# Graph convolutions on one Trainium2 core: 28 of 784 edge tiles fetched row by row from SyncE and ScalarE, and a ring of 72 slots

## The reference, cut to what matters

```python
def gcn_conv(x, W, b, src, dst, num_nodes):
    h = x @ W
    s = jnp.concatenate([src, loop]); d = jnp.concatenate([dst, loop])
    dinv = rsqrt(deg)
    msg = h[s] * (dinv[s] * dinv[d])[:, None]
    return jax.ops.segment_sum(msg, d, num_segments=num_nodes) + b
...
x = gcn_conv(layernorm(x), W1, b1, src, dst, 6250)
x = relu(x)
x = gcn_conv(x, W2, b2, src, dst, 6250)
```

## Time and profile before

| | us |
|---|---|
| runs | 4734.35, 4722.5, 4726.0 |
| median | 4726.0 |
| the profiled execution's own time | 4731.23 |
| its span | 4729.4 |
| mean granted TensorE clock | 0.743 of full speed |

### The profile page before, as it was taken

The page is one execution under the profiler, slowest core; times in us unless marked ns, Lnnn a source line. Parts: engine busy times, 40 slices in busy tenths (PEclk is TensorE's granted clock), DMA queues, the critical chain, the costliest instruction groups (busy, mean ns, idle before and its releaser), DMA issues. The chain is left out here.

```text
span 4729.4 us, 52933 instructions
## 1 busy us (share of the span) xinstructions
PE 2773.6 (59%) x12432; PEld 2169.6 (46%) x12432; DVE 2355.0 (50%) x5207; ACT 743.6 (16%) x1703; POOL 2645.2 (56%) x2784
## 2 busy tenths in 40 slices
PE   1333344433233333444548989968887877844998
PEld 0333333333233333333437744446666666632665
DVE  5533333333433333333645344448777777864344
ACT  0200000000000000000324422223333333312222
POOL 2777777777477777777440042147777777741000
PEclk9755666556655556666669999978888888875999
DMA  5122222222222222222323355444444444430000
GB/s 112 44 59 53 53 53 53 53 53 53 62 53 53 53 53 53 53 53 51 107 98 111 104 187 190 181 142 138 138 139 138 138 138 134 138 98 23 16 16 23
DMA packets 200796, 410.20 MB, mean 87 GB/s; under 512 B 51652, under 2 KB 125012, under 8 KB 193589
## 3 DMA queue, kind: packets, MB, share of 16 engines
q0 software_dynamic: 102144, 246.72, 19.3%
q1 hardware_dynamic: 98356, 160.05, 10.5%
HBM read 305.82 MB, written 104.44 MB: 87 GB/s over the span
## 5 line engine op out<-in xcount | busy, mean ns | idle before, releaser
L657 POOL DMA_INDIRECT ring<-t_gcn,idx x1568 | 1479.5, 944 | 545.0 <-issue 476.9
L683 PE MATMUL psum<-ring,big 128*128 x3328 | 770.7, 421 | 1281.7 <-SPq L666 1261.3
L683 PEld LDWEIGHTS psum<-ring,big 128*128 128x128 f32 x3328 | 707.0, 320 | 1345.3 <-issue 1344.5
L700 DVE TENSOR_TENSOR big<-big,psum 128x128 f32 x1664 | 480.6, 289 | 1257.3 <-PE psum L683 1065.0
L1509 POOL DMA_INDIRECT xs_ring<-t_msg,idx x832 | 801.5, 963 | 381.4 <-issue 252.5
L1637 PE MATMUL psum<-xs_ring,a_hot 128*128 128x264 f32 x1456 | 410.1, 442 | 0.0
L1637 PEld LDWEIGHTS psum<-xs_ring,a_hot 128*128 128x128 f32 x1456 | 332.8, 229 | 75.3
L1393 PE MATMUL psum<-big,a_xnt 128*128 128x512 f32 x784 | 354.4, 595 | 0.5 <-ACT a_xnt L1365 0.5
L1298 POOL DMA_INDIRECT a_back<-t_y,m_addr x98 | 97.7, 997 | 439.2 <-POOLq L1102 280.8
L831 ACT ACTIVATE m_xa<-big,dinv 128x128 f32<-128x128 f32 x49 | 19.4, 400 | 2028.3 <-PEq L643 2028.3
L412 DVE TENSOR_TENSOR big<-dloc,psum 128x1024 f32<-128x1024 f32 x210 | 254.8, 1214 | 26.3 <-PEq L709 13.1
(11 more groups left out here) (378 smaller groups left out, 3927.1 us busy)
## 6 DMA issues: line engine op xcount, KB each, us to landing
t_msg<-a_rows SPq DMA_DIRECT2D x49, 1056.0 KB, 3.9
a_near<-t_near SPq DMA_DIRECT2D x52, 512.0 KB, 4.1
ring<-t_gcn,idx POOLq DMA_INDIRECT x1568, 2.5
m_xin<-t_tok SPq DMA_DIRECT2D x105, 128.0 KB, 2.1
t_y<-m_yb SPq DMA_DIRECT2D x105, 128.0 KB, 2.1
xs_ring<-t_msg,idx POOLq DMA_INDIRECT x832, 2.8
xs_ring<-in_x SPq DMA_DIRECT2D x7, 896.0 KB, 11.1
t_gcn<-big SPq DMA_DIRECT2D x2, 3136.0 KB, 12.5
```

What stands on the lines that cost most here:

```text
L657: g.indirect_dma_start(out=ring[:, q % 4 * 8 + j, :], out_offset=None, in_=t_gcn[conv], in_offset=bass.IndirectOffsetOnAxis(ap=idx1[:, q * ...
L683: t.matmul(ps[j % 4][:, 0:HID], hot[q % 2][:, j, :], ring[:, at[j], :], start=True, stop=True).then_inc(s_used.sem, 1)
L700: v.tensor_tensor(a_n, a_n, ps[j % 4][:, 0:HID], ALU.add).then_inc(s_added.sem, 1)
```

## The change

The ring of each convolution grows from 32 to 72 slots, 9 halves, and four slots of its own follow. In each period of 56 edge tiles the 28th and the 56th are no longer gathered by POOL. SP fetches the 28th and ACT the 56th: it reads the tile's 128 source indices into SBUF, loads them eight at a time into registers and issues one DMA of one row for each edge, 128 to a tile, 14 tiles to an engine and convolution. Each has two slots in turn. When the last row has landed it raises `s_c` (SP) or `s_e` (ACT).

POOL waits on constants, at step counts that hold wherever the node tiles change, and signals one semaphore for each half. PE waits for those itself, once in each of the first 98 half turns, for the half of fetches with the half turn's own number. The tables `freed` and `fetch` go; `slot` is worked out with more vector operations on one partition. Buffers of the projection move to a narrower scope.

```diff
-RING = 32
+HALF_RING = 9
+RING = 8 * HALF_RING
+LONE = 56
+LONES = ETP // LONE
...
-                    v.memset(freed[:, 0:3], 0).then_inc(c.sem, c.up())
-                    v.tensor_copy(freed[:, 3:HALVES], krow[:, 0:(HALVES - 3) * 8].rearrange("p (h s) -> p h s", s=8)[:, :, 0]).then_inc(c.sem, c.up())
...
-                    v.tensor_scalar(fetch[:], slot[:].rearrange("p (q s) -> p q s", s=8)[:, :, 7], 3, None, ALU.arith_shift_right).then_inc(c.sem, c.up())
-                    v.wait_ge(c.sem, c.value())
-                    v.tensor_scalar(slot[:], slot[:], RING - 1, None, ALU.bitwise_and).then_inc(c.sem, c.up())
+                    whole(slot[:], 911.0, turn[:])
+                    whole(slot[:], 1171.0, period[:])
...
+                    v.scalar_tensor_tensor(within[:], period[:], -float(LONE), slot[:], ALU.mult, ALU.add).then_inc(c.sem, c.up())
+                    v.tensor_scalar(period[:], period[:], 1, None, ALU.bitwise_and).then_inc(c.sem, c.up())
...
+                    v.tensor_tensor(slot[:], slot[:], period[:], ALU.add).then_inc(c.sem, c.up())
...
-                    ring = sb(f"ring{conv}", [P, RING, HID], F32, cv)
+                    ring = sb(f"ring{conv}", [P, RING + 4, HID], F32, cv)
+                    lone_idx = [sb(f"lone{conv}_{k}", [1, 2, P], I32, cv) for k in range(2)]
...
+                    def lone_tile(k, i):
+                        return i * LONE + (k + 1) * LONE // 2 - 1
...
                     def _(g):
...
                         for q in range(HALVES):
-                            if q >= 4:
-                                g.load([freed_to], freed[0:1, q:q + 1])
-                                g.reg_alu(freed_at, freed_to, 0, ALU.max)
-                                g.wait_ge(s_used.sem, s_used.base + g.snap(freed_at, min_val=0, max_val=STEPS) + 16)
-                                g.nop(nofuse=True)
+                            if q >= HALF_RING:
+                                g.wait_ge(s_used.sem, s_used.base + min(8 * (q - HALF_RING) + 7 + NT, STEPS) + 16)
                             for j in range(8):
-                                g.indirect_dma_start(out=ring[:, q % 4 * 8 + j, :], out_offset=None, in_=t_gcn[conv],
-                                                     in_offset=bass.IndirectOffsetOnAxis(ap=idx1[:, q * 8 + j:q * 8 + j + 1], axis=0)
-                                                     ).then_inc(s_row[q % 4 * 8 + j].sem, 16)
+                                at = q % HALF_RING * 8 + j
+                                if q * 8 + j not in lone:
+                                    g.indirect_dma_start(out=ring[:, at, :], out_offset=None, in_=t_gcn[conv],
+                                                         in_offset=bass.IndirectOffsetOnAxis(ap=idx1[:, q * 8 + j:q * 8 + j + 1], axis=0)
+                                                         ).then_inc(s_row[q % HALF_RING].sem, 16)
+
+                    def lone_rows(engine, k):
+                        node_at = [engine.alloc_register(f"lone{conv}_{k}_{j}") for j in range(8)]
+
+                        def fetch_indices(i):
+                            t = lone_tile(k, i)
+                            engine.dma_start(lone_idx[k][:, i % 2, :], src[t:t + 1, :]).then_inc(s_known[k].sem, 16)
+
+                        fetch_indices(0)
+                        for i in range(LONES):
+                            engine.wait_ge(s_known[k].sem, s_known[k].base + 16 * i + 16)
+                            if i >= 2:
+                                engine.wait_ge(s_used.sem, s_used.base + lone_tile(k, i - 2) + NT + 16)
+                            for e in range(P):
+                                if e % 8 == 0:
+                                    engine.load(node_at, lone_idx[k][0:1, i % 2, e:e + 8])
+                                row = engine.snap(node_at[e % 8], min_val=0, max_val=NPAD - 1)
+                                engine.dma_start(ring[e:e + 1, RING + 2 * k + i % 2, :], t_gcn[conv][bass.ds(row, 1), :]).then_inc(s_came[k].sem, 16)
+                            if i + 1 < LONES:
+                                fetch_indices(i + 1)
+                            engine.wait_ge(s_came[k].sem, s_came[k].base + 16 * P * (i + 1))
+                            engine.sem_inc((s_c, s_e)[k].sem, 1)
 
                     @b.sync
                     def _(sp):
-                        for q in range(HALVES):
-                            for j in range(8 * (q % 4), 8 * (q % 4) + 8):
-                                sp.wait_ge(s_row[j].sem, s_row[j].base + q // 4 * 16 + 16)
-                            sp.sem_inc(s_c.sem, 1)
+                        lone_rows(sp, 0)
+
+                    @b.scalar
+                    def _(a):
+                        lone_rows(a, 1)
...
                         for q in range(2 * TURNS):
                             t.load(slot_of, slot[0:1, q * 8:q * 8 + 8])
-                            t.load([half_of], fetch[0:1, q:q + 1])
-                            t.reg_alu(half_at, half_of, 0, ALU.max)
                             t.wait_ge(s_hot.sem, s_hot.base + q + 1)
-                            t.wait_ge(s_c.sem, s_c.base + t.snap(half_at, min_val=0, max_val=HALVES - 1) + 1)
+                            if q < HALVES:
+                                gathers = 8 * (q // HALF_RING + 1) - sum(lone_tile(k, i) // 8 in range(q % HALF_RING, q + 1, HALF_RING)
+                                                                          for k in range(2) for i in range(LONES))
+                                t.wait_ge(s_row[q % HALF_RING].sem, s_row[q % HALF_RING].base + 16 * gathers)
+                                if q % (LONE // 8) == lone_tile(0, 0) // 8:
+                                    t.wait_ge(s_c.sem, s_c.base + q * 8 // LONE + 1)
+                                if q % (LONE // 8) == lone_tile(1, 0) // 8:
+                                    t.wait_ge(s_e.sem, s_e.base + q * 8 // LONE + 1)
```

More of the change, by code:

```diff
@@ L230, in gnn_ffn_kernel @@
             near = sb("near", [P, SCH, P], BF16, ph)
+            turn, period, within, last = (sb(f"at_{k}", [1, PSTEPS], I32, ph) for k in ("turn", "period", "within", "last"))
             vector_steps = []
@@ L324, in _, with whole @@
                         v.sem_inc(s_d.sem, 1)
-                    v.memset(freed[:, 0:3], 0).then_inc(c.sem, c.up())
-                    v.tensor_copy(freed[:, 3:HALVES], krow[:, 0:(HALVES - 3) * 8].rearrange("p (h s) -> p h s", s=8)[:, :, 0]).then_inc(c.sem, c.up())
+                    def whole(src, by, out):
+                        v.tensor_scalar(out, src, by, None, ALU.mult).then_inc(c.sem, c.up())
+                        v.wait_ge(c.sem, c.value())
+                        v.tensor_scalar(out, out, 16, None, ALU.arith_shift_right).then_inc(c.sem, c.up())
@@ new lines, in _ @@
+                    v.tensor_scalar(period[:], period[:], 1, None, ALU.bitwise_and).then_inc(c.sem, c.up())
+                    v.wait_ge(c.sem, c.value())
+                    v.scalar_tensor_tensor(slot[:], turn[:], -float(RING), slot[:], ALU.mult, ALU.add).then_inc(c.sem, c.up())
+                    v.tensor_scalar(last[:], within[:], float(LONE - 1), None, ALU.is_equal).then_inc(c.sem, c.up())
+                    v.tensor_scalar(within[:], within[:], float(LONE // 2 - 1), None, ALU.is_equal).then_inc(c.sem, c.up())
@@ new lines, in _ @@
+                    v.wait_ge(c.sem, c.value())
+                    v.tensor_tensor(within[:], within[:], last[:], ALU.add).then_inc(c.sem, c.up())
+                    v.tensor_tensor(period[:], period[:], slot[:], ALU.subtract).then_inc(c.sem, c.up())
+                    v.wait_ge(c.sem, c.value())
+                    v.scalar_tensor_tensor(period[:], period[:], float(RING), within[:], ALU.add, ALU.mult).then_inc(c.sem, c.up())
+                    v.wait_ge(c.sem, c.value())
+                    v.scalar_tensor_tensor(period[:], last[:], 2.0, period[:], ALU.mult, ALU.add).then_inc(c.sem, c.up())
@@ L433, in gnn_ffn_kernel @@
                 deg = sb("deg", [P, NT], F32, dg)
+                w1 = sb("w1", [P, KD, HID], F32, dg)
+                xn = [sb(f"xn{k}", [P, D], F32, dg) for k in range(4)]
+                xnt = [sb(f"xnt{k}", [P, D], F32, dg) for k in range(4)]
                 first_i = sb("first_c", [P, FT], I32, dg)
@@ L643, in gnn_ffn_kernel @@
                 with nc.Block() as b, ExitStack() as cv:
-                    ring = sb(f"ring{conv}", [P, RING, HID], F32, cv)
+                    ring = sb(f"ring{conv}", [P, RING + 4, HID], F32, cv)
+                    lone_idx = [sb(f"lone{conv}_{k}", [1, 2, P], I32, cv) for k in range(2)]
+                    s_came = [sig(f"s_came{conv}_{k}") for k in range(2)]
+                    s_known = [sig(f"s_known{conv}_{k}") for k in range(2)]
+                    def lone_tile(k, i):
+                        return i * LONE + (k + 1) * LONE // 2 - 1
@@ L646, in _ @@
                     @b.gpsimd
                     def _(g):
```

(25 more changed lines are left out.)

10 lines of the change are left out of this document (2 added, 8 removed).

## The result

| | before | after |
|---|---|---|
| median | 4725.7 us | 4802.8 us |
| all runs | 4722.5 to 4734.35 | 4798.97 to 4831.67 |
| ratio | | 1.0173 (95%: 1.0132 to 1.0215) |
| span of the profiled execution | 4729.4 us | 4799.7 us |

A second series beside more runs of the kernel before gave 1.0147 (1.0130 to 1.0164).

What follows compares the result with a forecast made beforehand. POOL's gather issue bounds the kernel; after the change SP and ACT do. A convolution: 2.3 + 1100.4 + 33.8 + 0.4 = 1136.9 us against 986.5, +150.4, twice +300.8: 5027 us on the median's scale, range 4900 to 5190.

Steps and rivals of the forecast that it cites:

- What bounds the kernel, and what the change takes away: Both convolutions: POOL's issue rate, 1.248 us a gather, is the bound; 28 gathers fewer save 34.9 us each.
- The tail behind POOL's last gather: Convolution's end: PE's wait for the last half leaves seven half turns, 36.6 us instead of 9.05, 27.6 more.
- What a lone tile costs: SP or ACT fetching one tile row by row: 76.3 us, 78.6 with the turn to the next tile.
- The yardstick: SP's 128-row DMAs in the experts' phase: register operation, move and issue of 44, 29 and 338 ns, taken for one row.
- T: Time from one row-by-row tile of SP or ACT to its next: 78.6 us, against POOL's 67.4 a period.
- The tail behind the last lone tile: Convolution's end: seven half turns follow ACT's tile 783, 33.8 us plus 0.4.
- Nothing else is in their way: Convolutions: SP and ACT fetch 14 tiles each, one after the other, never held by PE's steps for a slot.
- The first stall: Near a convolution's start, if POOL stays the bound: POOL waits once for tile 27, T - 52.4 us.
- rows somewhat cheaper: Rival for SP's and ACT's fetches: T from 67 to 74, 4740 to 4898 us; chance 0.07.
- issue is cheap: Rival for the convolutions: POOL stays the bound, not slower, 4711 us with T under 53; chance 0.05.
- rows hold each other up: Rival: SP and ACT issuing at once take 0.43 us an issue, T = 90.3, 5354 us; chance 0.12.
- Parts with one answer: Smaller parts: slot table 8 to 10 us on DVE, hidden; PE's lost load, SP's dropped relay and moved buffers cost nothing.

Runs made afterwards that it cites:

- the probe: Kernel before plus a block of SP work alone behind the second convolution, with register-addressed DMAs of 1, 4, 16 and 128 rows; one-row issue 0.228 us.

## Why the prediction was right or wrong

**What bounds the kernel, and what the change takes away: right.** POOL's rate stayed at 1.2487 us in the changed kernel between its stalls, and 14 fewer tiles in the kernel with periods of 112 brought just 14 x 1.248. In four other kernels, one of them without lone tiles, it was 1.2508 to 1.2512; why is open, and it is 2 us a convolution.

**The tail behind POOL's last gather: right.** +27.6 us a convolution was reckoned, 28.5 measured in the changed kernel and 29.0 with no lone tiles.

**What a lone tile costs: wrong, and this is the larger part of the error.** The step that failed is "I keep 0.338, which lies between the one-row issues and the shortest", and with it the bound of 0.32 below. The yardstick was a DMA of 128 rows. The two one-row rows that I set beside it, 0.36 and 0.35, were issues to fixed addresses that came first in a burst or behind another, and a single issue of that kind says little: 16 in a row at fixed addresses took 0.252. The sign that I had named for this, an issue under 0.25 us, is there: 0.225 on SP and 0.214 on ACT. Per tile the rows took 128 x 0.416 = 53.2 us for my 67.2, so -14.0; the loads 16 x 0.85 (with the slower first row behind each) for my 16 x 0.57, so +4.5; the turn between tiles 2.9 for 2.3. T: 78.6 - 14.0 + 4.5 + 0.6 = 69.7; the mean of the intervals is 69.6. The mistakes in the row and in the load had opposite signs, and the measured 69.6 lies below every bound that I had for the forecast. The range began at T = 74; I named the cheaper cases (0.07 and 0.05) and left them out. In the sum T alone makes 14 x 9.0 = 126 us a convolution too many; the next mistake, of the other sign, took 14.5 of these away.

**The tail behind the last lone tile: wrong, 14.5 us a convolution.** With T = 69.6 my own sum gives 2.3 + 14 x 69.6 + 34.2 = 1010.9 us; measured are 1024.5. The step that failed is "ACT's last tile is number 783, in the last half, so the tail of seven half turns comes after it". In my own picture both engines' fourteenth tiles come in together, and PE stands then at the half of SP's, 755, which is half 94. Ten half turns are left, not seven. Three more at 4.83 us make 14.5, and the sum becomes 1025.4. The trace has it so: PE's last wait for SP ends in half turn 94, 49.2 us before the end. Where the last wait stood elsewhere the tail followed it, seven half turns and 33.8 us with SP's first tile taken by POOL, four and 20.3 with waits by table.

**"Nothing else is in their way": right for SP, wrong for ACT, and it cost nothing.** SP's pauses between tiles are 2.1 to 3.0 us throughout. ACT began its third tile 15 us late (the gap up to 391.53) and then waited for PE's steps again in most periods, with pauses of up to 4.5 us. But PE never waited for ACT.

**The first stall.** I had reckoned it, T - 52.4 = 17.1 us, for the rival in which POOL is the bound; POOL stood for 16.0. That is near by luck. I had POOL stand at half 6 for SP's first tile, but by the code of the change POOL waits for nothing before half 9, and only 1.6 us were lost there. The 16 us come at half 13, before the 102nd gather: POOL needs half turn 10, and PE stood there for SP's second tile until 139.6 us after the start.

**The sign and the chances.** Slower was right, and for the reason given: T is above POOL's 67.4 us. But the margin was 2.2 us and not 11. Of the rivals, "rows somewhat cheaper" came true by its T and by its time, with a chance of 0.07. The rival "issue is cheap" stays within 0.3% up to T = 66.8. With 16 registers a load T is about 66.4, and the kernel came out at 1.0017, inside the 0.3% as that rival says. So it was a much nearer miss than its 0.05: 2.7 us of T. The last, that rows hold each other up, is excluded by the probe (0.228 alone, 0.225 beside ACT).

**The rule of issue.** The Trainium skill, in DMA: Bandwidth & Descriptors, section "Issuing engines are not separate DMA queues", has the issue as "usually small relative to the DMA itself". That held no better than I said: a row every 0.416 us makes 53 us for 64 KB. My number for it was too high, the direction right.

**Parts with one answer.** The slot table's 14 operations ran from 67.58 to 79.3 us, 11.7 us for my 8 to 10, as half of them took 1.08 us and not 0.61. DVE still stood for 10.59 us before the next block where it had stood 21.97: hidden. POOL's stalls were to be "some 10 us in each period"; they were 2.2.

## What to carry to other kernels

When the price of an added operation comes from its neighbour in the trace, ask what in the neighbour scales. Here the issue of a DMA got cheaper by a third from 128 rows to one. And the helpers' 69.6 us stood against a limit of 67.4, so a price that is 30% off decides what is gained and what is lost.

A conservative wait, in the step order instead of the need, cost nothing on the way while POOL did all the gathers, and its whole lead at the end. Look at what is left to do when the last transfer lands, and do it for each engine that brings one: the tail to count starts at the item that the consumer stands at, not at the last item in order.

A helper that fetches ahead should not be given an item near the start of the pipeline, where it has no lead. One that is a little slower than the rest never wins it.

## What the runs showed of the hardware

The issue of a register-addressed DMA on SP takes 0.228 us for 1 row of 512 bytes, 0.253 for 4, 0.315 for 16 and 0.333 for 128. On ACT it takes 0.214 for one row, but 0.448 for the first behind each load of registers. Such DMAs of 1, 4, 16 and 128 rows bring 1, 4, 16 and 16 small packets beside their rows.

With its register work a row comes every 0.416 us on SP and every 0.377 on ACT, with both at it. POOL's gathers kept their 1.249 us beside them in the changed kernel and in the one with periods of 112.

A load of eight registers on SP takes 0.53 to 0.78 us, depending on what was issued before it, and a load of sixteen 1.23, so half as many loads cost a fifth less time in all.
